# Attention units of one core: where the fp32 products stand among the projections, and where the last output sum and the gate stand

## The chip, the core and the metric

The kernel runs on one core of one Trainium2 chip. The metric is the device time of one execution in microseconds (us). Of three runs the median is 936.8 us, the lowest 935.56 and the highest 937.04.

## What is computed

Four blocks act one after the other on x of shape 64 x 32 x 256 (64 sequences of 32 rows), each added to x: a transformer block with modulation, a GRU, a block attention and an oscillator network. The change touches the transformer block alone, and of it the attention:

```python
x1 = _ln(x) * (1.0 + scale1) + shift1
qkv = (x1 @ qkv_w + qkv_b).reshape(Bc, Tc, 3, H, DH)      # H = 16 heads, DH = 128
q, k, v = (qkv[:, :, 0], qkv[:, :, 1], qkv[:, :, 2])
attn = jnp.einsum('bthd,bshd->bhts', q, k) * scale
attn = jax.nn.softmax(attn, axis=-1)
attn_out = jnp.einsum('bhts,bshd->bthd', attn, v).reshape(Bc, Tc, INNER)
x = x + gate1 * (attn_out @ out_w + out_b)
x2 = _ln(x) * (1.0 + scale2) + shift2
h = jax.nn.gelu(x2 @ ffn_w1 + ffn_b1, approximate=False)
x = x + gate2 * (h @ ffn_w2 + ffn_b2)
```

## The kernel before, in words

The 2048 rows are cut in NG = 4 groups of GT = 512 rows (16 sequences), the 16 heads in NU = 4 units of HU = 4 heads. The attention is software-pipelined over the 16 units (group by group): step U finishes unit U and does the projections of unit U + 1. Each engine has its own program, and semaphores alone tie them.

**TensorE.** A step is a list written out by hand, `STEP` (L477), gone through by `run` (L483). Its entries are:
- `q`, `k` and `v` (`proj`, L390): a projection. Each is a block of six fp32r matmuls of 512 columns (`three`, L349: high times high, low times high, high times low, for two halves of the features). The blocks alternate between two PSUM banks, so a block waits until the block two before it has been copied out (`act_evac`, `dve_evac`).
- `S` (`scores`, L413): the scores of one head, 16 small fp32 matmuls on 32 columns of the array, 32 records in the trace.
- `PV` (`pv`, L425): probabilities by values of one head, four fp32 matmuls of 128 columns, 8 records. It waits for the softmax of its unit at the first head, and for the copies of earlier products.
- `Y` (`head_sum`, L436): the output projection of one head, added up over all 16 heads in two PSUM banks; six fp32r matmuls.

The mean and the variance for the layer norms are one fp32 matmul each by a matrix of 1/256 (two records; four in the first group). `attention` (L549) puts them at the head of a step: `ln_mean(g + 1)` and `ln_var(g + 1)` in steps 0 and 1 of a group; in the last group those of the second norm, `l2_mean(0)`, `l2_var(0)`, `l2_mean(1)`, and `l2_var(1)` at the head of the last step. The last step, `LAST` (L480), has no projections but the first three blocks `U` of the feed-forward (`up`, L512), and the fourth.

**ScalarE** (`attention`, L885) copies out q (`query`, L808) and half of v (`value`, L817), takes the exponential (`exp`, L823), and writes the high part of each head's product (`out_high`, L827). The norm's square, root and high part (`ln_square`, `ln_sqrt`, `high`, or `l2_square`, `l2_sqrt`, `m_high`) stand between `query` 1 and `query` 2.

**VectorE** (`attention`, L1274) copies out k (`key`, L1127) and the other half of v (`value`, L1134), and writes the low part of each product (`out_low`, L1140). Softmax is `soft_a` (L1151: maximum and difference, out of PSUM), `soft_b` (L1159: sum, reciprocal, and the multiplication of the probabilities at L1165, whose operands both lie in SBUF) and `soft_c` (L1167: four transposes of 32 partitions each into the block-diagonal operand `BD` of `PV`). In a step they stand as `soft_a`, `value` 1, `soft_b`, `value` 3, `soft_c`. At the end of a group's last step stands `gate` (L1216): it waits for the last `Y` and adds the gated sum to x, four instructions. The norm's part (`ln_center`, `ln_recip`, `low`, or `l2_center`, `l2_recip`, `m_low`) stands between `key` 1 and `key` 2.

**GpSimd** splits the weights of the units 1 to 3 into high and low parts in the first 101 us (`split`, L1684), and does the modulation of the next group's input (`modulate`, L1667: one multiplication by the reciprocal root, then four of half the size), which starts when VectorE's reciprocal is done. In the last steps it also prepares the feed-forward: the sum of the squares (`sum_squares`, L1704) and the low parts of both weights (`ffn_low`, L1731); the order is written out from L1762 on. `ffn_low(f2_lo, ...)` stands right behind `l2_sum_squares(1)`.

Each engine works through its own list in order: whatever waits holds up all that stands behind it on that engine.

Of the kernel before, what the change touches and what calls it, by code (L numbers as in the profile page):

```python
# [15 lines left out]
NG = 4  # L16
# [83 lines left out]
def build(nc, xT, cond, ada_w, qkv_w, out_w, ffn_w1, ffn_w2, w_ih, w_hh, wk, wo, coup, vecs, out):  # L100
# [20 lines left out]
    with ctx:  # L121
# [224 lines left out]
        def _(pe):  # L346
# [113 lines left out]
            def idle_matmuls(n):  # L460
                for _ in range(n):
# [14 lines left out]
                     ("S", 2), ("v", 0), ("S", 3), ("v", 1), ("v", 2), ("v", 3)]  # L476
            STEP = [("q", 0), ("k", 0), ("q", 1), ("k", 1), ("S", 0), ("q", 2), ("k", 2), ("S", 1), ("PV", 0), ("q", 3),  # L477
                    ("PV", 1), ("k", 3), ("Y", 0), ("S", 2), ("PV", 2), ("Y", 1), ("PV", 3), ("S", 3), ("v", 0),
                    ("Y", 2), ("v", 1), ("v", 2), ("v", 3), ("Y", 3)]
            LAST = [("L", 1), ("U", 0), ("U", 1), ("PV", 0), ("PV", 1), ("U", 2), ("Y", 0), ("PV", 2), ("Y", 1), ("PV", 3),  # L480
                    ("U", 3), ("Y", 2), ("Y", 3)]

            def run(order, U, u, g):  # L483
# [3 lines left out]
                for kind, i in order:  # L487
                    if kind == "PV":
                        pv(U, i)
                    elif kind == "Y":  # L490
                        head_sum(U, u, i, g)
                    elif kind == "U":
                        up(i)
                    elif kind == "L":
                        l2_var(i)
                    elif kind == "S":
                        scores(n, i)
                    else:
                        proj(n, ng, un, (kind, i))
# [48 lines left out]

            def attention(g, last):  # L549
                for u in range(NU):  # L550
                    U = NU * g + u
                    if not last and u == 0:
                        ln_mean(g + 1)
                    if not last and u == 1:
                        ln_var(g + 1)

                    if last and u == 0:
                        l2_mean(0)
                    if last and u == 1:
                        l2_var(0)  # L560
                    if last and u == 2:
                        l2_mean(1)
                    run(LAST if last and u == NU - 1 else STEP, U, u, g)

            for g in range(NG):
                attention(g, g == NG - 1)

# [222 lines left out]
        def _(act):  # L790
# [94 lines left out]
            def attention(g, last):  # L885
                for u in range(NU):
# [3 lines left out]
                    if project:  # L890
                        query(n, un, 0)
                        query(n, un, 1)
                    if u == 0 and not last:
                        ln_square(g + 1)
# [8 lines left out]
                    if u == 2 and last:  # L903
                        m_high(0)
                    if not project:
                        break
                    query(n, un, 2)
                    out_high(U, u, 0)
                    query(n, un, 3)
                    out_high(U, u, 1)  # L910
                    if u == 2 and last:
                        l2_square(1)
                    out_high(U, u, 2)
                    out_high(U, u, 3)
                    value(n, 0)
# [3 lines left out]
            def last_unit():  # L919
                U, u = NU * NG - 1, NU - 1  # L920
                l2_sqrt(1)
                hidden(0)
                hidden(1)
                out_high(U, u, 0)
                out_high(U, u, 1)
                hidden(2)
                out_high(U, u, 2)
                out_high(U, u, 3)
                hidden(3)

# [173 lines left out]
        def _(dve):  # L1104
# [61 lines left out]

            def soft_c(U):  # L1167
                soft_wait(U, "norm")
                dve.wait_ge(pv_done, 1 + 4 * U)
                for j in range(BT):  # L1170
                    js = slice(j * T, j * T + T)
# [102 lines left out]
            def attention(g, last):  # L1274
                for u in range(NU):
# [3 lines left out]
                    if project:  # L1279
                        key(n, un, 0)  # L1280
                        key(n, un, 1)
                    if u == 0 and not last:
                        ln_center(g + 1)
                    if u == 1 and not last:
                        ln_recip(g + 1)
                    if u == 2 and not last:
                        low(g + 1)
                    if u == 0 and last:
                        l2_center(0)
                    if u == 1 and last:  # L1290
                        l2_recip(0)
                    if u == 2 and last:
                        m_low(0)
                        l2_center(1)
                    if not project:
                        break
                    key(n, un, 2)
                    out_low(U, u, 0)
                    out_low(U, u, 1)
                    key(n, un, 3)  # L1300
                    out_low(U, u, 2)
                    out_low(U, u, 3)
                    soft_a(n)
                    value(n, 1)
                    soft_b(n)
                    value(n, 3)
                    soft_c(n)
                    if u == NU - 1:
                        gate(g)

            def last_unit():
                U, u = NU * NG - 1, NU - 1
                hidden_low(0)
                out_low(U, u, 0)
                out_low(U, u, 1)
                l2_recip(1)
                hidden_low(1)
                out_low(U, u, 2)
# [605 lines left out]
```

## Time and profile before

| | |
|---|---|
| median of three runs | 936.8 us |
| the profiled execution, its own time | 935.23 us |
| its span, first to last instruction | 933.5 us |
| TensorE matmul busy | 909.0 us, 97% of the span |
| TensorE weight load busy | 767.8 us, 82% |
| VectorE busy | 613.0 us, 66% |
| ScalarE busy | 415.2 us, 44% |
| GpSimd busy | 258.2 us, 28% |
| chain that ended last | PE 85%, DVE 9%, ACT 3%, issue 2%, DMA 1% |
| the line that holds most of the chain | L355 (the fp32r matmuls), 42% |
| granted TensorE clock, mean | 0.995 of full speed |

The span in 40 slices of 23 us, busy share in tenths:

```profile
PE   7999999999999999999999999999997899999998
DVE  5545645455455455545577885677777988888887
POOL 0655400020000200013502424333214543333333
PEclk9999999999999999999999999999999899999999
```

The attention fills the slices 3 to 21 (from 42.5 to 489.5 us). The profiler's engines are PE (TensorE matmul), PEld (its weight loads), DVE (VectorE), ACT (ScalarE), POOL (GpSimd). Records of matmuls overlap, since they are pipelined: the distance from one start to the next tells what a matmul costs, its own length does not.

### The profile page before, as it was taken

Reading aid. Unit: us, or ns where it says so; the run is one execution under the profiler, and the core shown is the slowest. Engines: PE = TensorE matmul, PEld = TensorE weight load, DVE = VectorE, ACT = ScalarE, POOL = GpSimd, SP = SyncE. Lnnn points to the kernel's source line nnn. Section 1 sums busy time; section 2 is a strip of 40 time slices with the busy share of each in tenths; the row PEclk is TensorE's granted clock in tenths of the full one; section 3 lists DMA queues with packets and bytes.
Section 4 is the critical chain, followed back from the end, with each engine's and each line's share of the span. In section 5 each row is a group of like instructions: output and inputs, shape, how many; then the busy total and the mean of one; then the engine's idle time right before and its main releaser. Section 6 shows DMA issues by size and latency. Waiting matters only on the chain.

```text
span 933.5 us, 18576 instructions
## 1 busy us (share of the span) xinstructions
PE 909.0 (97%) x7254; PEld 767.8 (82%) x7254; DVE 613.0 (66%) x1706; ACT 415.2 (44%) x1147; POOL 258.2 (28%) x344
## 2 busy tenths in 40 slices
PE   7999999999999999999999999999997899999998
PEld 6787887888878888788887778899985599999997
DVE  5545645455455455545577885677777988888887
ACT  3233322333222422224355664555544666666665
POOL 0655400020000200013502424333214543333333
PEclk9999999999999999999999999999999899999999
DMA  8122000000000000110005000000000000000000
GB/s 298 58 74 75 24 1 1 1 2 1 2 1 1 2 1 1 46 46 2 2 1 192 1 0 1 1 2 1 1 2 1 1 2 24 1 24 2 24 2 24
DMA packets 5432, 22.01 MB, mean 24 GB/s; under 512 B 608, under 2 KB 736, under 8 KB 4960
## 3 DMA queue, kind: packets, MB, share of 16 engines
q1 hardware_dynamic: 5344, 20.82, 6.4%
q8 instruction: 57, 0.93, 0.4%
q14 instruction: 31, 0.25, 0.1%
HBM read 18.72 MB, written 2.10 MB: 22 GB/s over the span
## 4 chain that ended last, share of the span: by engine, by line
PE 85%; DVE 9%; ACT 3%; issue 2%; DMA 1%; SPq 0%; POOL 0%; POOLq 0%; DVEq 0%
PE ps L355 42%; PE ps L747 8%; PE ps L432 7%; PE ps L751 7%; PE ps L615 6%; PE ps L746 5%; PE ps L605 3%; PE ps L421 3%; PE ps L617 3%; DVE g_lo L1214 1%; DVE BD L1172 1%; DVE m_lo L1208 1%; DVE frs L1186 1%; DMA BD<-qkv_w 1%; PE ps L622 1%
## 5 line engine op out<-in xcount | busy, mean ns | idle before, releaser
L1142 DVE SCALAR_TENSOR_TENSOR o_lo<-ps,vec,o_hi 128x512 fp32r<-128x512 f32 x64 | 47.9, 750 | 106.4 <-ACT o_hi L830 106.4
L355 PE MATMUL ps<-x_hi,W_hi 128*128 128x512 f32 x256 | 108.6, 424 | 3.4 <-DVE qk L1131 3.0
L355 PE MATMUL ps<-x_lo,W_hi 128*128 128x512 f32 x256 | 100.2, 391 | 0.0
L814 ACT ACTIVATE qk<-ps,vec 128x512 f32<-128x512 f32 x64 | 44.0, 688 | 126.1 <-PE ps L355 126.1
L747 PE MATMUL ps<-rk_th,cpc 128*128 128x128 f32 x512 | 99.0, 296 | 1.1 <-ACT rk_th L1080 1.0
L355 PE MATMUL ps<-x_hi,W_lo 128*128 128x512 f32 x256 | 100.0, 391 | 0.0
L830 ACT ACTIVATE o_hi<-ps,vec 128x512 fp32r<-128x512 f32 x64 | 43.9, 689 | 110.4 <-PE ps L432 110.4
L1131 DVE TENSOR_SCALAR qk<-ps,vec 128x512 f32<-128x512 f32 x64 | 47.4, 740 | 64.9 <-PE ps L355 64.9
L747 PEld LDWEIGHTS ps<-rk_th,cpc 128*128 128x128 f32 x512 | 72.9, 193 | 9.6 <-ACT rk_th L1080 7.3
L746 PE MATMUL ps<-rk_th,cpc 128*128 128x64 f32 x512 | 78.7, 256 | 0.0
L615 PE MATMUL ps<-ht,hh 128*128 128x128 f32 x512 | 77.1, 283 | 0.8 <-DVE ht L1468 0.7
L746 PEld LDWEIGHTS ps<-rk_th,cpc 128*128 128x128 f32 x512 | 73.1, 193 | 0.0
L615 PEld LDWEIGHTS ps<-ht,hh 128*128 128x128 f32 x512 | 66.0, 191 | 7.5 <-DVE ht L1468 4.6
L432 PE MATMUL ps<-BD,V 128*128 128x128 f32 x512 | 70.3, 281 | 0.0
L1080 ACT ACTIVATE rk_th<-rk_q 128x64 f32<-128x64 f32 x192 | 44.5, 253 | 54.0 <-DVE rk_q L1630 22.5
L432 PEld LDWEIGHTS ps<-BD,V 128*128 128x128 f32 x512 | 64.4, 191 | 4.1
L751 PE MATMUL ps<-rk_Z,ident 128*128 128x128 f32 x384 | 64.3, 290 | 0.0
L355 PEld LDWEIGHTS ps<-x_hi,W_hi 128*128 128x128 f32 x256 | 48.2, 188 | 16.3 <-DVE qk L1131 5.0
L355 PEld LDWEIGHTS ps<-x_hi,W_lo 128*128 128x128 f32 x256 | 48.2, 188 | 10.3 <-issue 2.2
L355 PEld LDWEIGHTS ps<-x_lo,W_hi 128*128 128x128 f32 x256 | 48.0, 188 | 10.5
L355 PE MATMUL ps<-W_hi,x_hi 128*128 128x512 f32 x128 | 51.8, 404 | 0.0
L355 PE MATMUL ps<-o_hi,wo_hi 128*128 128x512 f32 x128 | 51.5, 402 | 0.0
(257 smaller groups left out, 2144.1 us busy)
## 6 DMA issues: line engine op xcount, KB each, us to landing
stage<-qkv_w SPq DMA_DIRECT2D x6, 768.0 KB, 4.3
stage<-out_w SPq DMA_DIRECT2D x4, 512.0 KB, 3.8
f_raw<-ffn_w SPq DMA_DIRECT2D x2, 1024.0 KB, 4.8
xorig<-xT SPq DMA_DIRECT2D x1, 2048.0 KB, 8.1
out<-xtb SPq DMA_DIRECT2D x4, 512.0 KB, 3.1
x_all<-xT SPq DMA_DIRECT2D x1, 1536.0 KB, 15.3
ada_sb<-ada_w SPq DMA_DIRECT2D x1, 1024.0 KB, 10.1
BD<-qkv_w SPq DMA_DIRECT2D x1, 768.0 KB, 6.6
```

What stands on the lines that cost most here:

```text
L355: r = pe.matmul(out_, lhsT, rhs, start=first and i == 0, stop=last and i == n - 1)
L421: r = pe.matmul(ps[j * T:j * T + T, SB, (i * HU + h) * T:(i * HU + h) * T + T], qk[:, 0, h % 2, t], qk[:, 1, h % 2, t], start=True, stop=True)
L432: r = pe.matmul(ps[:, OB[h % 2], i * P:i * P + P], V[:, i, h * DH:h * DH + DH], BD[:, i * HU + h, :], start=True, stop=True)
L615: return pe.matmul(ps[:, bank[c], 0:2 * B], hh[:, k, ms], h_.unsqueeze(1).to_broadcast([P, 2, B]), start=k == 0, stop=k == KC - 1)
L746: return pe.matmul(ps[:, RK_BANK[k % 2][c], 0:B], w, th, start=first, stop=last)
L747: return pe.matmul(ps[:, RK_BANK[k % 2][c], 0:2 * B], w, twice(th), start=first, stop=last)
L751: pe.matmul(ps[:, RK_BANK[k % 2][c], 0:2 * B], ident[:, :], twice(rk[z][:, c, :]), start=True, stop=False)
L814: act.activation(qk[:, 0, h % 2, :], ps[:, PJ[0], :], ACT.Identity, bias=col("qkv_b", HU * u + h)).then_inc(act_evac, 1)
L830: act.activation(o_hi[:, h % 2, :], ps[:, OB[h % 2], :], ACT.Identity, bias=col("qkv_b", 2 * HEADS + HU * u + h)).then_inc(ohi_done, 1)
L1080: act.activation(rk[f"th{k % 2}"][:, c, :], rk[src][:, c, :], ACT.Tanh).then_inc(rk_act, 1)
L1131: dve.tensor_scalar(qk[:, 1, h % 2, :], ps[:, PJ[1], :], col("qkv_b", HEADS + HU * u + h), None, ALU.add).then_inc(dve_evac, 1)
L1142: dve.scalar_tensor_tensor(o_lo[:, h % 2, :], ps[:, OB[h % 2], :], col("qkv_b", 2 * HEADS + HU * u + h), o_hi[:, h % 2, :].bitcast(F32), A ...
```

## The change

It puts the fp32 products of a step in two places: both first heads' products by values and scores after the fourth projection block, those of the other two heads after four more projections and two output sums. The fourth output sum `Y` 3 of a unit goes into the next step, after `k` 1 there, and the norm's matmul with it, right behind. On ScalarE and VectorE the orders follow: the norm's work goes behind `query` 3 and `key` 3, `out_high` and `out_low` of the heads 0 and 1 come ahead of `query` 2 and `key` 2, `l2_square(1)` goes behind `out_high` 3, two of the four transposes go ahead of `value` 3, and `gate` goes into the next group's first step, behind `key` 1. The last step changes in the same way.

```diff
-            STEP = [("q", 0), ("k", 0), ("q", 1), ("k", 1), ("S", 0), ("q", 2), ("k", 2), ("S", 1), ("PV", 0), ("q", 3),
-                    ("PV", 1), ("k", 3), ("Y", 0), ("S", 2), ("PV", 2), ("Y", 1), ("PV", 3), ("S", 3), ("v", 0),
-                    ("Y", 2), ("v", 1), ("v", 2), ("v", 3), ("Y", 3)]
-            LAST = [("L", 1), ("U", 0), ("U", 1), ("PV", 0), ("PV", 1), ("U", 2), ("Y", 0), ("PV", 2), ("Y", 1), ("PV", 3),
-                    ("U", 3), ("Y", 2), ("Y", 3)]
+            STEP = [("q", 0), ("k", 0), ("q", 1), ("k", 1), ("previous Y", 3), ("norm", 0), ("PV", 0), ("PV", 1), ("S", 0), ("S", 1),
+                    ("q", 2), ("k", 2), ("q", 3), ("k", 3), ("Y", 0), ("Y", 1), ("PV", 2), ("PV", 3), ("S", 2), ("S", 3),
+                    ("v", 0), ("v", 1), ("Y", 2), ("v", 2), ("v", 3)]
+            LAST = [("previous Y", 3), ("norm", 0), ("U", 0), ("U", 1), ("PV", 0), ("PV", 1), ("U", 2), ("Y", 0), ("Y", 1),
+                    ("PV", 2), ("PV", 3), ("U", 3), ("Y", 2), ("Y", 3)]
...
+                    elif kind == "previous Y":
+                        if U:
+                            head_sum(U - 1, (u - 1) % NU, i, (U - 1) // NU)
+                    elif kind == "norm":
+                        norm_sum(u, g, g == NG - 1)
...
+            def norm_sum(u, g, last):
+                if last:
+                    (l2_mean, l2_var)[u % 2](u // 2)
+                elif u == 0:
+                    ln_mean(g + 1)
+                elif u == 1:
+                    ln_var(g + 1)
```

ScalarE, a step (the norm's lines between are the same as before):

```diff
                     if project:
                         query(n, un, 0)
                         query(n, un, 1)
+                    if not project:
+                        break
+                    out_high(U, u, 0)
+                    out_high(U, u, 1)
+                    query(n, un, 2)
+                    query(n, un, 3)
                     if u == 0 and not last:
                         ln_square(g + 1)
...
-                    if not project:
-                        break
-                    query(n, un, 2)
-                    out_high(U, u, 0)
-                    query(n, un, 3)
-                    out_high(U, u, 1)
+                    out_high(U, u, 2)
+                    out_high(U, u, 3)
                     if u == 2 and last:
                         l2_square(1)
-                    out_high(U, u, 2)
-                    out_high(U, u, 3)
```

VectorE, a step:

```diff
+                    if u == 0 and g:
+                        gate(g - 1)
+                    if not project:
+                        break
+                    out_low(U, u, 0)
+                    out_low(U, u, 1)
                     if u == 0 and not last:
                         ln_center(g + 1)
+                    if u == 0 and last:
+                        l2_center(0)
+                    key(n, un, 2)
+                    key(n, un, 3)
...
                     out_low(U, u, 2)
                     out_low(U, u, 3)
                     soft_a(n)
                     value(n, 1)
                     soft_b(n)
+                    soft_c(n, range(2))
                     value(n, 3)
-                    soft_c(n)
-                    if u == NU - 1:
-                        gate(g)
+                    soft_c(n, range(2, BT))
```

In the last step ScalarE's `out_high` 0 and 1 come ahead of `hidden(0)`, and `out_high` 2 and 3 ahead of `hidden(2)`; VectorE's `hidden_low(0)` comes behind `l2_recip(1)`.

## Rows read from the trace of the kernel before

**Rows 1.** Chain that ended last, in order of time, a plain unit: start us, us, what

```profile
322.11 0.39 PE ps L421 x32
322.49 13.85 PE ps L355 x60
...
340.06 1.09 PE ps L432 x8
...
349.93 0.39 PE ps L421 x32
```

**Rows 2.** The same chain, a unit with a norm's matmul

```profile
436.87 8.41 PE ps L355 x36
445.28 0.86 PE ps L367 x2
```

**Rows 3.** The same chain, the last unit

```profile
477.62 1.78 PE ps L432 x16
479.40 2.99 PE ps L355 x12
...
485.56 8.20 PE ps L355 x36
```

**Rows 4.** Stretches: length, busy us (x) of PE, PEld, DVE, ACT, POOL, PEclk, DMA share, GB/s

```profile
157.60:165.34 7.74, 6.73 (x27) 4.62 (x26) 5.80 (x9) 1.38 (x2) 0.00 (x0) 1.00 0.00 0
416.40:422.83 6.43, 6.43 (x27) 4.70 (x26) 3.00 (x5) 1.92 (x3) 0.87 (x1) 1.00 0.36 146
93.32:107.47 14.16, 14.15 (x69) 11.11 (x61) 9.92 (x13) 4.90 (x7) 9.87 (x8) 1.00 0.12 38
```

**Rows 5.** Timeline of DVE, end of the first group: start, us, what, count [idle before]

```profile
157.05 2.89 DVE L1172 STREAM_TRANSPOSE BD<-Pr 32x512 f32<-32x512 f32 x4
160.05 0.75 DVE L1224 SCALAR_TENSOR_TENSOR Pr<-ps,vec,ada 128x512 f32<-128x512 f32 x1
...
162.96 0.74 DVE L1131 TENSOR_SCALAR qk<-ps,vec 128x512 f32<-128x512 f32 x1
```

**Rows 6.** Timeline of PE, a unit with the norm's root

```profile
212.27 0.39 PE L355 MATMUL ps<-W_hi,x_hi 128*128 128x512 f32 x1
```

**Rows 7.** Timeline of ACT, the same unit

```profile
193.52 1.28 ACT L802 ACT_TABLE_LOAD   x1
...
209.73 0.60 ACT L821 ACTIVATE V<-ps 128x512 f32<-128x512 f32 x1 [1.29 <-PE ps L355]
...
211.64 0.63 ACT L825 ACTIVATE Pr<-Pr 128x512 f32<-128x512 f32 x1
```

**Rows 8.** Timeline of DVE, the same unit

```profile
195.54 3.35 DVE L1121 RECIPROCAL rs<-rs 128x512 f32<-128x512 f32 x1 [0.61 <-ACT rs L802]
...
212.47 0.69 DVE L1138 COPY V<-ps 128x512 f32<-128x512 f32 x1 [1.92 <-PE ps L355]
213.08 0.68 DVE L1161 TENSOR_REDUCE sm<-Pr 128x16 f32<-128x512 f32 x1
...
214.08 0.69 DVE L1165 TENSOR_TENSOR Pr<-Pr,sm 128x512 f32<-128x512 f32 x1
```

**Rows 9.** Timeline of POOL, the same unit: the modulation

```profile
198.97 2.39 POOL L1670 TENSOR_TENSOR xc<-xc,rs 128x1024 f32<-128x1024 f32 x1 [29.19 <-DVE rs L1121]
201.44 4.20 POOL L1675 TENSOR_TENSOR xc<-xc,ada 128x512 f32<-128x512 f32 x4
```

**Rows 10.** Timeline of POOL, then of DVE, at the end of the second unit

```profile
98.67 2.40 POOL L1689 TENSOR_TENSOR wo_lo<-stage,wo_hi 128x1024 fp32r<-128x1024 f32 x1
...
99.36 2.27 DVE L1165 TENSOR_TENSOR Pr<-Pr,sm 128x512 f32<-128x512 f32 x1
```

**Rows 11.** Timeline of ACT, then of POOL, in the fifteenth unit

```profile
459.34 1.05 ACT L856 ACTIVATE fsq<-fc 128x1024 f32<-128x1024 f32 x1
...
460.47 1.29 POOL L1706 TENSOR_TENSOR fsq<-fsq 128x512 f32<-128x512 f32 x1 [9.98 <-ACT fsq L856]
461.72 4.57 POOL L1734 TENSOR_TENSOR f_lo<-f_raw,f_hi 128x2048 fp32r<-128x2048 f32 x1
```

More of the change, by code:

```diff
@@ L493, in run @@
                         up(i)
-                    elif kind == "L":
-                        l2_var(i)
+                    elif kind == "previous Y":
[3 more added lines that the diff above has]
+                        norm_sum(u, g, g == NG - 1)
                     elif kind == "S":
@@ L547, in down @@
                     r.then_inc(down_done, 1)
[L549 to L566, printed above, removed]
+            def norm_sum(u, g, last):
[5 more added lines that the diff above has]
+                    ln_var(g + 1)
+            for U in range(NU * NG):
+                run(LAST if U == NU * NG - 1 else STEP, U, U % NU, U // NU)
             down(0)
@@ L921, in last_unit @@
                 l2_sqrt(1)
+                out_high(U, u, 0)
+                out_high(U, u, 1)
                 hidden(0)
                 hidden(1)
-                out_high(U, u, 0)
-                out_high(U, u, 1)
-                hidden(2)
                 out_high(U, u, 2)
                 out_high(U, u, 3)
+                hidden(2)
                 hidden(3)
@@ L1165, in soft_b, with soft_c @@
                 dve.tensor_tensor(Pr[:, :, :], Pr[:, :, :], sm[:, :].unsqueeze(2).to_broadcast(whole), ALU.mult).then_inc(soft, 1)
-            def soft_c(U):
+            def soft_c(U, blocks=range(BT)):
                 soft_wait(U, "norm")
                 dve.wait_ge(pv_done, 1 + 4 * U)
-                for j in range(BT):
+                for j in blocks:
                     js = slice(j * T, j * T + T)
@@ L1287, in attention @@
                         low(g + 1)
-                    if u == 0 and last:
-                        l2_center(0)
                     if u == 1 and last:
@@ L1294, in attention @@
                         l2_center(1)
[L1295 to L1300, printed above, removed]
                     out_low(U, u, 2)
@@ L1305, in attention @@
                     soft_b(n)
+                    soft_c(n, range(2))
                     value(n, 3)
-                    soft_c(n)
-                    if u == NU - 1:
-                        gate(g)
+                    soft_c(n, range(2, BT))
             def last_unit():
                 U, u = NU * NG - 1, NU - 1
-                hidden_low(0)
                 out_low(U, u, 0)
@@ L1316, in last_unit @@
                 l2_recip(1)
+                hidden_low(0)
                 hidden_low(1)
```

## The prediction

> **What bounds the kernel.** I read the page first: TensorE is busy for 97% of the span and holds 85% of the chain. So I went on to the chain in order of time, inside the attention. Through a plain unit it runs on TensorE without a break, 27.82 us from one unit's last scores to the next's [rows 1]. What shortens it is less on TensorE, or fewer waits; the other engines count only where TensorE waits for them.
>
> The reader is to see in [rows 1] that a piece's price depends on what it follows. 36 fp32r matmuls behind a `PV` take 8.20 us, 0.228 each [rows 3]. The 60 behind an `S` take 13.85 where 60 x 0.228 is 13.67, and 36 behind one take 8.41, 0.21 more than 8.20 [rows 2]. A `PV` behind `S` takes 1.09, two in a row 1.78, 0.89 each [rows 3], so 0.20 less. Leaving scores costs about 0.2 us; `S` itself is 0.39.
>
> **The change part by part.** *The regrouping.* Four departures from scores in a unit become two. The new unit, in pieces that rows show: behind the last `S` again 60 (`v` 0, `v` 1, `Y` 2, `v` 2, `v` 3, `q` 0, `k` 0, `q` 1, `k` 1, `Y` 3), 13.85; two pairs of `PV`, 2 x 1.78; 36 behind `S`, 8.41; four `S`, 1.55. Sum 27.37, against 27.82: 0.45 less, in 15 units 6.7 us. No row shows `S` behind `S`. Within one head 32 records follow each other in 0.39 us, and the next head is more of them: I take nothing extra. Nothing less either, since that 0.39 holds no departure; above, a full departure, 0.2 in 30 places, 6.0 us.
>
> *The norm's matmul* moves and is kept, 0.86 us [rows 2]. It now stands between `Y` and `PV`. The 36, the matmul and the 24 that follow make up about 0.04 more than 13.85 and 0.86, so at most 0.4 us for nine places goes or comes: I count zero.
>
> *The last step* has its `PV` in two pairs (1.78 as the row's pair, so nothing) and loses a wait ahead of `Y` 0: 12 matmuls took 2.99 [rows 3] where 12 x 0.228 is 2.73. ScalarE now writes the high parts ahead of `hidden(0)`. Gain 0.3.
>
> *The gate.* It waits for `Y` 3 at a group's end, and VectorE runs it from 160.05 to 162.96, with the next `key` 0 behind it [rows 5]; `k` 1 waits for that copy. The stretch from the norm's matmul to the first scores is 7.74 us in such a step and 6.43 where no gate stands [rows 4]: 1.31, in three places 3.9 us. Behind `key` 1 the gate begins when `Y` 3 ends, about 7.0 us into the unit, and ends at 9.9. Behind it wait `out_low` 0, `out_low` 1 and `ln_center`, up to 12.6; `key` 2 is wanted at 13.4 (seven blocks of 1.36, the norm's 0.9, two `PV` and two `S` 2.6, a departure 0.2, and 0.2 until a copy begins), `Y` 0 at 16, which also needs the two sum banks that the gate has read. So it is hidden, with 0.8 us to spare; without that cover it would cost TensorE what it cost before.
>
> *The third unit's 60* took 14.16 [rows 4] against 13.85, behind a late softmax: 0.3 may go, but see the rule below; I count it.
>
> Gains together: 6.7 + 0.3 + 3.9 + 0.3 = 11.2 us.
>
> *The new waits.* The last projection of `v` leaves its bank through VectorE's `value` 3, now behind `soft_b` and two transposes (half of 2.89 [rows 5], 1.45). The next `k` 0 needs that bank. I work it through for the steps with the norm's root (the second of each group), counting from the end of block `k` 3:
> - A copy begins 0.20 after its block ends (212.27 to 212.47 [rows 6, 8]). So `query` 3 begins at -1.16, the table load at about -0.45, the reciprocal 2.02 later [rows 7, 8], at 1.57, and the modulation on GpSimd 3.43 after that [rows 8, 9], at 5.0. Its first instruction is followed after 2.47 by four in 4.20 [rows 9]: the last of them runs from 10.6 to 11.7.
> - On TensorE `Y` 0 and `Y` 1 (2.7), `PV` 2 and 3 (1.8), `S` 2 and 3 (0.8) and `v` 0 (1.6) end at 6.9. The copy begins at 7.1, the exponential 1.91 later with a table load between [rows 7], ends 9.6; the sum begins at 9.7 and the multiplication L1165 1.00 later [rows 8], at 10.7.
> - Undisturbed it ends at 11.4, two transposes at 12.8, `value` 3 at 13.5; `k` 0 is wanted at 13.7 (five blocks behind `v` 0). No wait, with 0.2 to spare.
>
> But two instructions that read SBUF twice over collide: at 99.36 the multiplication took 2.27 instead of 0.69 and ended at 101.63, 0.56 after GpSimd's (98.67 + 2.40) [rows 10]. In the steps above it comes 0.1 us after GpSimd's last one began. Held to 11.7 it ends at 12.2, `value` 3 at 14.4: `k` 0 waits 0.7. Three groups (units 6, 10, 14; in the first, GpSimd is still at the weights): 2.2 us. Had it come 0.1 earlier, it would take its turn between two of them: nothing. I take the 2.2, by the step's own arithmetic, and keep zero as the other end.
>
> *The fifteenth unit.* `l2_square(1)` is moved behind `out_high` 3, so that it ends about 6.4 after `k` 3 (1.05 long); the sum of squares takes 1.29, and the low part of the second weight, one instruction of 4.57 us [rows 11], runs from 7.7 to 12.3. No table load here, so the multiplication is ready at 10.0, held to 12.3, ends at 12.9; two transposes, 14.3; `value` 3, 15.0. The last step's `U` 0 needs it and is wanted at 14.5 (four blocks, `Y` 3 and 0.86): 0.5 us. It is 2.3 us deep inside the other instruction, so I count it; the other end is zero.
>
> Moved without a price: `high`, `low`, `m_high`, `m_low` (done at about 17 of 27 us, wanted by the next unit); the transposes, which `PV` 0 now wants some 6 us after they end; no DMA is moved, and SP's queue waits for projections, which come earlier.
>
> **Sum.** 11.2 - 2.2 - 0.5 = 8.5 us. The profiled execution took 935.2 and would take 926.7; the median stands 1.6 above it, so 928.3.
>
> **A rule weighed.** The row shows a TENSOR_TENSOR of GpSimd blocking [rows 10]. The Trainium skill (SBUF — State Buffer, Who interferes with whom) says that a VectorE instruction with two SBUF inputs contends with any GpSimd instruction that reads SBUF, and that the loser blocks to the end. This trace agrees for the pair shown; a TENSOR_SCALAR against it no row here shows.
>
> **The rivals.**
> 1. *The multiplication slips in ahead* of GpSimd's last instruction. For it: the distance is 0.1 us over a chain of 12 us. Then 2.2 comes back: 926.1. Chance 0.28.
> 2. *GpSimd's scalar form blocks too.* In the second unit I put the multiplication at about 97.8, when GpSimd is at the instruction just ahead of that at 98.67. Held to 98.6, it ends at 99.2, `value` 3 comes 0.6 late, the third unit waits as long: 928.9. Were it 0.9 later still, it would meet the next one and cost 2 more. By the rule just named this is what happens. Chance 0.20.
> 3. *Scores behind scores cost a departure:* 6.0 more, 934.3. Against it: the 32 even records. Chance 0.05.
> 4. *The gate's wait comes back* behind `out_low` and `key` 2, 3 x 1.3: 932.2. It needs VectorE 0.8 us later than counted. Chance 0.05.
> 5. *Slower.* `value` 3 behind the two transposes holds `k` 0 in all 15 units. It decides where VectorE is later by more than 0.5 us in plain steps and 0.2 in those with the root; it turns the sign at 11.2 / 15 = 0.75 of wait a unit, so some 1.3 us late. If both transposes and the multiplication met such delays everywhere (1.6 us as in [rows 10], less the 0.5), that is 1.1 x 15 = 16.5 us against 11.2: 942. Against it: GpSimd is idle in most units. Chance 0.04.
> 6. *It does less than it says*, TensorE waiting elsewhere for about what it gains, within 0.2%: chance 0.05.
>
> **How the numbers follow.** The forecast has 0.33. The likeliest is 928.3. Measurement can tell about 0.2% (1.9 us) from no change. Faster by more than that: the forecast and rivals 1, 2, 4 and, at 934.3 just so, most of 3: 0.90. Same 0.06, slower 0.04. For the range: down to rival 1 less the 0.4 of the norm, the 0.5 of the fifteenth unit and part of the clock's play; up past rival 2 with its further 2 us, towards rival 4. The clock's play is this: the page's granted clock shows one slice of 8, from 723 to 747 us, in a later stage where TensorE waits; 0.1 to 0.2 of those 23 us is 2 to 4 us at the lower rate, and shifted by 8 us the dip may fall better or worse, an estimate of 1 to 2 us. 924.3 to 932.
>
> **What would show it.** Chain: `PV` x16 twice and `S` x64 at 0.78 in a unit; 27.4 for a plain unit; no `Pr L1224` in it. Stretch ahead of the first `S` in a group's first step: no wait of TensorE for `qk L1131`. Waits: three of 0.7 on `V L1138` ahead of `k` 0, one of 0.5 ahead of `U` 0; on VectorE three L1165 of 1.5 us and one near 3. A plain unit over 27.6 would prove the regrouping wrong; waits of TensorE in plain units, rival 5.

## The result and the profile after

The changed kernel takes **924.4 us** (922.4 to 927.1 in four executions) against 936.9 us (of four executions; the 936.8 above is of three): ratio 0.9872, interval 0.9859 to 0.9885, a gain of 12.5 us where 8.5 were forecast. The profiled execution took 922.4 us, with a span of 920.7; before it was 935.2 and 933.5.

Two measures serve below. A *chain piece* is read as before the prediction. A *start-to-start* length runs from the first record of one piece to the first of the next; in these a plain unit before is 27.82 us. The *attention* is the time from the first record of scores to the last record of a product, start to start: 456.09 us before, 443.06 after. The difference is 13.0 us, so the whole gain lies there; the rest adds and takes a few tenths (448.7 us of the trace lie behind the attention's last product, before 448.2), and the spans end 12.8 apart.

The page after, span, busy times and the slices' row of the granted clock:

```profile
span 920.7 us, 18591 instructions
PE 901.2 (98%) x7254; PEld 771.7 (84%) x7254; DVE 615.9 (67%) x1706; ACT 414.4 (45%) x1147; POOL 260.0 (28%) x344
...
PEclk9999999999999999999999999999998999999999
```

TensorE runs the same 7254 matmuls in 12.8 us less and is still busy nearly throughout. The slice of lower clock now lies at 690 to 713 us; it was at 723 to 747.

The chain in order of time, a plain unit after (start us, us, what), which answers to [rows 1]:

```profile
312.62 0.69 PE ps L421 x50
313.31 13.87 PE ps L355 x60
327.18 1.78 PE ps L432 x16
328.96 0.69 PE ps L421 x50
329.66 8.38 PE ps L355 x36
338.04 1.78 PE ps L432 x16
339.82 0.69 PE ps L421 x50
```

From 312.62 to 339.82 it is 27.20 us with a wait of 0.05 in its 60 (they follow a root); start to start a plain unit is 27.16, **0.66 less** than before. The two runs of scores take 0.69 each (all 64 matmuls; the chain lists 50 of them), and the forecast had 0.78. One head by itself takes 0.39 start to start, the pair 0.69, so the second head's scores behind the first's cost 0.31, not 0.39.

The chain in a group's first step, which answers to the first of [rows 4]:

```profile
146.80 13.82 PE ps L355 x60
160.62 0.86 PE ps L367 x2
161.48 1.78 PE ps L432 x16
```

TensorE does not wait. The timeline of VectorE over the same time shows the gate behind a `key` copy, with TensorE past it:

```profile
159.30 0.75 DVE L1126 TENSOR_SCALAR qk<-ps,vec 128x512 f32<-128x512 f32 x1 [1.97 <-PE ps L355]
160.66 0.75 DVE L1219 SCALAR_TENSOR_TENSOR Pr<-ps,vec,ada 128x512 f32<-128x512 f32 x1 [0.61 <-PE ps L355]
```

The waits by engine and line show the three waits for a `key` copy (before 3.0 us) gone, and two others inside the attention (us in total, times, the longest): at the last step's `U` 0, and at the first step's `k` 1:

```profile
PE ps L355 <- DVE V L1133: 0.6, 1, 0.6
...
PE ps L355 <- DVE qk L1126: 0.3, 1, 0.3
```

The second is a cost of the change that the forecast does not have. The chain shows it:

```profile
45.95 0.76 DVE qk L1126
...
46.75 1.66 PE ps L355 x6
```

VectorE's copies of the first unit stand ahead of its loop, and there all four transposes are still behind `value` 3 (`soft_c(0)`); the `key` copy comes behind them. Before, the norm's matmul of four records stood at the head of the step, between `v` 3 and `q` 0, and gave time; now it stands behind `k` 1, and no `Y` 3 of a unit ahead is there. So the first step is 0.07 us shorter than before, from its last scores to the next unit's, where a plain one is 0.66 shorter: a loss of **0.6 us**. (The 0.3 of the list is what the engine is idle by its records, which overlap.)

The two collisions that the forecast counted. The timeline after of VectorE, then of GpSimd: a unit with the norm's root (the first row of each) and the fifteenth unit (the second of each). *Blocked* means that an instruction takes longer because the other engine's is under way:

```profile
208.04 0.69 DVE L1160 TENSOR_TENSOR Pr<-Pr,sm 128x512 f32<-128x512 f32 x1
...
456.40 2.88 DVE L1160 TENSOR_TENSOR Pr<-Pr,sm 128x512 f32<-128x512 f32 x1
...
204.96 4.69 POOL L1671 TENSOR_TENSOR xc<-xc,ada 128x512 f32<-128x512 f32 x4
...
454.12 4.61 POOL L1730 TENSOR_TENSOR f_lo<-f_raw,f_hi 128x2048 fp32r<-128x2048 f32 x1
```

In the first the multiplication ran in its 0.69 us and GpSimd's group of four took 4.69 in place of 4.20 [rows 9]: its last instruction began at 208.10, 0.06 **behind** the multiplication, and it was the one blocked (1.54 us instead of 1.05). The same order, by 0.05 to 0.06, stands in the other two such units. TensorE's 60 matmuls took 13.79, 13.78 and 13.81 there, against 13.73 in a plain unit: 0.2 us in all where 2.2 were counted. In the fifteenth unit the multiplication came 2.3 us deep inside the other and took 2.88.

### The profile page after: what moved, and what is told of

Read it like the earlier page. It is cut to its first block, busy times and chain, and to the rows that moved or that the text cites. A ratio compares the mean times of both kernels' runs of the same rounds, so it can differ in the third digit from the quotient of the medians.

```text
span 920.7 us, 18591 instructions
## 1 busy us (share of the span) xinstructions
PE 901.2 (98%) x7254; PEld 771.7 (84%) x7254; DVE 615.9 (67%) x1706; ACT 414.4 (45%) x1147; POOL 260.0 (28%) x344
## 4 chain that ended last, share of the span: by engine, by line
PE 87%; DVE 8%; ACT 3%; issue 1%; POOL 0%; POOLq 0%; DVEq 0%; ACTq 0%
PE ps L355 43%; PE ps L742 8%; PE ps L746 6%; PE ps L610 6%; PE ps L432 6%; PE ps L741 5%; PE ps L600 3%; PE ps L612 3%; PE ps L421 2%; PE ps L617 1%; DVE g_lo L1209 1%; DVE m_lo L1203 1%; PE ps L367 1%; DVE frs L1181 1%; PE ps L362 1%
## 5 line engine op out<-in xcount | busy, mean ns | idle before, releaser
L355 PE MATMUL ps<-x_hi,W_hi 128*128 128x512 f32 x256 | 102.0, 399 | 0.7 <-DVE x_lo L1254 0.4
L432 PEld LDWEIGHTS ps<-BD,V 128*128 128x128 f32 x512 | 62.1, 191 | 6.1 <-issue 4.3
L432 PE MATMUL ps<-BD,V 128*128 128x128 f32 x512 | 62.3, 275 | 0.0
L355 PEld LDWEIGHTS ps<-x_lo,W_hi 128*128 128x128 f32 x256 | 48.1, 188 | 10.3
L746 PEld LDWEIGHTS ps<-rk_Z,ident 128*128 128x128 f32 x384 | 50.6, 192 | 0.3 <-DVE rk_Z L1609 0.3
```

What stands on the lines that cost most here:

```text
L355: r = pe.matmul(out_, lhsT, rhs, start=first and i == 0, stop=last and i == n - 1)
L432: r = pe.matmul(ps[:, OB[h % 2], i * P:i * P + P], V[:, i, h * DH:h * DH + DH], BD[:, i * HU + h, :], start=True, stop=True)
L746: pe.matmul(ps[:, RK_BANK[k % 2][c], 0:2 * B], ident[:, :], twice(rk[z][:, c, :]), start=True, stop=False)
```

## The experiments

Three questions stand: what the regrouping is worth and why it gave more than its pieces; whether moving the gate and `Y` 3 gives anything; and whether the collisions of VectorE and GpSimd are what the forecast took them for. My theory after the result, as the expectations have it: a sum of parts, 0.66 us in each of 15 units from the regrouping, and 3.9 us from the gate's move on top. The other view: the regrouping alone gives it all. Attention lengths, start to start, of every profiled execution:

| kernel | attention us | less than before |
|---|---|---|
| before | 456.09 | |
| the change, three executions | 443.06, 444.13, 442.97 | 13.0, 12.0, 13.1 |
| gate moved alone | 451.87 | 4.2 |
| regrouping alone | 442.61 | 13.5 |
| the change, one pair of scores split | 448.57 | 7.5 |
| the change, transposes whole | 450.46 | 5.6 |
| the change, square earlier | 442.70 | 13.4 |
| the change, three small writes ahead of the product | 443.15 | 12.9 |
| the change, product made later | 446.12 | 10.0 |
| regrouping, `Y` 2 ahead of `v` 1 | 445.82 | 10.3 |
| regrouping, transposes whole | 445.59 | 10.5 |
| regrouping, square earlier | 441.86 | 14.2 |

### The change again

> The changed kernel once more, beside the others on one chip. Theory A (the gain is made of three sums that show in the trace: 0.66 us less in each of 15 units, 1.3 us in three steps with a gate, 0.3 in the third unit, less 0.8 of waiting ahead of U 0 in the last step): 13.0 us less inside the attention, ratio to before 0.986. Theory B (part of the median's gain is the clock's, since its four runs lie at 922.4, 922.7, 926.1 and 927.1): again two levels some 4 us apart, and a profile of a run at the upper level shows the loss behind the attention.

924.0 us (922.3 to 927.5 in four), ratio 0.9883 (0.9859 to 0.9908); a third series, run beside other kernels, is below. The profiled execution took longer, span 925.8. The stretches view of its first projections (length, PE busy, clock, DMA share, GB/s):

```profile
20.00:32.00 12.00, 9.18 (x76) 0.86 0.17 63
```

The granted clock is 0.86 in the mean there (a part of the stretch at the lower level, 1.2 GHz, the rest at 2.4), where both first profiles have 1.00: the first 24 matmuls took 7.26 us instead of 5.81, and attention began 2.1 us later. The attention is 1.1 longer, and what lies behind it 1.9 longer (450.6 us against 448.7); together these are the 5.1 between the spans. At the end of the second unit, the timeline of VectorE, then of GpSimd:

```profile
99.75 1.62 DVE L1160 TENSOR_TENSOR Pr<-Pr,sm 128x512 f32<-128x512 f32 x1
...
98.42 2.40 POOL L1685 TENSOR_TENSOR wo_lo<-stage,wo_hi 128x1024 fp32r<-128x1024 f32 x1
100.78 2.83 POOL L1666 TENSOR_TENSOR xc<-xc,rs 128x1024 f32<-128x1024 f32 x1
```

Here GpSimd, which follows a transfer, is ahead of the attention by more, and its next instruction holds the multiplication: 1.62 us instead of 0.69. It then took its turn as soon as the first had ended, and GpSimd's following one paid 0.43. The third unit's 60 matmuls took 14.75, 1.0 more than in a plain unit. This collision is worth a microsecond, and whether it happens varies: of the twelve profiled executions of the changed kernel and its variants (the gate moved alone left out) the second unit's multiplication was blocked in five. Expected were 13.0 us less inside the attention; it was 12.0, by this collision.

> The changed kernel once more. Theory A (startup shifts TensorE's first projection by up to 2 us against GpSimd's weight splitting, which the loads set): where the trace shows the first projection as late as 40.1 us (fourth scores), the second unit's multiplication meets GpSimd's split and the third unit's 60 matmuls take 14.7 us; where it is at 38, 13.8 us. Theory B: the level of a run is set by how long the clock is at half where TensorE is thin, near 715 and 730 us and in the first projection, 3.4 or 6.8 us each time.

925.4 us (923.1 to 928.9 in four), ratio 0.9896 (0.9871 to 0.992). The profiled one took 923.1; its third unit shows 13.79 and the three units with the root 13.79, 13.77 and 13.77: the multiplication at 209.16, GpSimd's last at 209.23. So the order of 0.06 us holds in all three profiles of this kernel; in each the multiplication begins 5.69 to 5.70 us behind the start of the last scores. The fourth scores began at 38.7 and the second unit did not collide, which agrees with the expectation. But a late start alone does not bring the collision: in the run with three small writes, below, they began at 39.8 and the stretch took 13.81, for there GpSimd waited longer for its transfer and came after the multiplication (99.86 against 99.77).

### The gate moved alone

```diff
# kernel before, VectorE
                         l2_center(1)
+                    if u == 0 and g:
+                        gate(g - 1)
...
                     soft_c(n)
-                    if u == NU - 1:
-                        gate(g)
```

> The kernel before with the gate alone moved: out of the end of a group's last step into the next group's first step, behind ln_center; scores, products and Y 3 stay where they were. Theory A: the wait of k 1 on the copy behind the gate goes in three places, 3.9 us less, about 933.0 where before is 936.9; a plain unit stays at 27.82 us. Rival (the gate only moves its wait: out_low 0, key 2 or the next Y 0 pay): within 1 us of before.

931.8 us (931.3 to 932.5), ratio 0.9962 (0.9947 to 0.9977). The chain in a group's first step:

```profile
158.90 0.86 PE ps L367 x2
159.76 5.48 PE ps L355 x24
165.24 0.39 PE ps L421 x32
```

The 24 matmuls run without a wait: start to start 5.98 where before it was 7.28, 1.30 in each of three places, 3.9 us. The third unit's 60 gave 0.3 more in this execution (13.85). A plain unit stays at 27.82. So the term of 3.9 us holds, taken by itself.

### The regrouping alone

```diff
# changed kernel
-            STEP = [("q", 0), ("k", 0), ("q", 1), ("k", 1), ("previous Y", 3), ("norm", 0), ("PV", 0), ...
+            STEP = [("norm", 0), ("q", 0), ("k", 0), ("q", 1), ("k", 1), ("PV", 0), ...
...
-                    ("v", 0), ("v", 1), ("Y", 2), ("v", 2), ("v", 3)]
+                    ("v", 0), ("v", 1), ("Y", 2), ("v", 2), ("v", 3), ("Y", 3)]
...
-                    if u == 0 and g:
-                        gate(g - 1)
...
                     soft_c(n, range(2, BT))
+                    if u == NU - 1:
+                        gate(g)
```

> The changed kernel with Y 3 and the norm's matmul back at the step's end and head and the gate back at the group's end: the regrouping alone. Theory A: a unit of 27.16 us, 15 x 0.66 = 9.9 us less, the three waits of 1.3 us for the copy behind the gate are there again, about 926.5 to 927.5. Rival (Y 3 in the next step is what makes room for the pairs): TensorE waits for out_low or the softmax in plain units, the unit stays above 27.5 us and the time above 931.

923.2 us (921.8 to 925.1), ratio 0.9868 (0.9846 to 0.989): **all of the gain, without `Y` 3's move and the gate's**. The attention is even 0.45 us shorter than with them, mostly since the first step's loss of 0.6 us is not there either. I had expected three waits of 1.3 us and 926.5 to 927.5: that was wrong. The timeline of VectorE at the end of the first group tells why no gate is felt:

```profile
151.51 0.69 DVE L1133 COPY V<-ps 128x512 f32<-128x512 f32 x1 [0.85 <-PE ps L355]
...
155.59 0.69 DVE L1133 COPY V<-ps 128x512 f32<-128x512 f32 x1 [0.32 <-PE ps L355]
156.31 1.44 DVE L1167 STREAM_TRANSPOSE BD<-Pr 32x512 f32<-32x512 f32 x2
157.86 0.75 DVE L1219 SCALAR_TENSOR_TENSOR Pr<-ps,vec,ada 128x512 f32<-128x512 f32 x1
...
160.77 0.74 DVE L1126 TENSOR_SCALAR qk<-ps,vec 128x512 f32<-128x512 f32 x1
```

The gate takes the same 2.9 us ahead of the `key` copy, but begins 1.35 us earlier against the matmuls (9.41 us behind the end of the last scores, before 10.76). `v` 1 stands ahead of `Y` 2, so that its copy and the softmax behind it come one block of 1.36 earlier, and two transposes are then already done ahead of `value` 3. `v` 3 itself ends no earlier. The 24 matmuls took 5.92, 5.92 and 5.89. Of the units with the root, the two whose 60 stand undivided took 13.73: with `Y` 3 behind `v` 3, `k` 0 comes 1.36 us later and `value` 3 has that much time to spare.

### Which part of the new order removes the gate's wait

```diff
# regrouping alone
-                    ("v", 0), ("v", 1), ("Y", 2), ("v", 2), ("v", 3), ("Y", 3)]
+                    ("v", 0), ("Y", 2), ("v", 1), ("v", 2), ("v", 3), ("Y", 3)]
```

> The regrouping alone with Y 2 ahead of v 1 again, as before the change. In the regrouping alone the gate at the group's end costs nothing: the stretch behind the norm's matmul takes 5.89 to 5.92 us. Theory A (v 1 ahead of Y 2 lets VectorE copy v 1 and finish the softmax 1.3 us earlier, so the gate is over when k 0's copy is wanted): with Y 2 first, value 1, the sum and the multiplication come 0.8 to 1.3 us later, and k 1 waits 0.3 to 1.0 us in the three steps with a gate. Rival (the split of the transposes alone did it): 5.9 us as before.

925.3 us, one execution. The chain ahead of the first scores of the second group:

```profile
158.28 0.76 DVE Pr L1219
...
159.68 0.76 DVE qk L1126
...
160.48 1.66 PE ps L355 x6
```

The gate is in the chain again and six matmuls (`k` 1) follow the copy; the 24 took 6.93, 6.94 and 6.93: 1.01 to 1.04 more in three places. Here the transposes come 1.36 later and end after `v` 3, so that `value` 3 waits for them.

```diff
# regrouping alone
                     soft_b(n)
-                    soft_c(n, range(2))
                     value(n, 3)
-                    soft_c(n, range(2, BT))
+                    soft_c(n)
```

> The regrouping alone with all four transposes behind value 3. Theory A: the gate begins 1.2 us later (at the end of transposes that start when value 3 ends), key 0 too, and k 1 waits about 1.0 us in each of the three steps with a gate (24 matmuls 6.9 us instead of 5.9); plain steps keep 27.16, since Y 3 stands between v 3 and q 0 here. Rival (the order of v 1 and Y 2 alone did it): 5.9 us as before.

926.9 us, one execution. The 24 matmuls took 7.18, 7.19 and 7.19: 1.3 more each. The wait at the fifteenth unit is gone in it, 0.8 less, and the attention is 3.0 longer, as 3.8 less 0.8 would have it. Either half of the order, undone, brings nearly the whole wait back, so both are needed where the gate isn't moved.

### Transposes whole, with `Y` 3 moved

The same edit on the changed kernel.

> The changed kernel with all four transposes behind value 3, as before the change. Theory A (the split spreads VectorE's load so that neither value 3 nor key 0 comes late): the four end about 0.7 us later than key 0 is wanted, k 1 waits for the bank about 0.3 us in every step, the unit goes from 27.16 to about 27.5, 4 to 5 us in all. Rival (value 3 comes earlier and k 0 gains what k 1 loses): the same within 1 us.

932.8 us, one execution. Now **every** unit waits. The chain, at the head of a plain unit:

```profile
358.59 0.71 DVE BD L1167
359.33 0.76 DVE qk L1126
360.14 1.89 PE ps L355 x7
```

`k` 1 waits for a `key` copy behind four transposes; the 60 matmuls took 14.33 to 14.35, 0.6 more in each of the 14 such stretches, twice what I had expected. That is 8.4 us; the wait at the last step's `U` 0 (0.8) is gone with it, and the attention is 7.4 longer than in the change. In the run before this, with `Y` 3 in its place, the same transposes cost plain units nothing (13.73). That is the price of the move of `Y` 3: it takes away 1.36 us of cover at the seam of every unit, and only the split of the transposes makes up for it. It is rival 5's mechanism, at a price of 0.6 a unit, just under the 0.75 that would have turned the sign.

### One pair of scores split

```diff
# changed kernel
-                    ("PV", 0), ("PV", 1), ("S", 0), ("S", 1), ("q", 2), ("k", 2), ...
+                    ("PV", 0), ("PV", 1), ("S", 0), ("q", 2), ("S", 1), ("k", 2), ...
```

> The changed kernel with the first pair of scores taken apart: S 1 behind q 2, all else as it is. Theory A, sharpened by the trace after (two S in a row take 0.69 us, not 2 x 0.39, and each stay apart also pays an entry of 0.07 and a departure of 0.15): 0.31 us more a unit, 15 x 0.31 = 4.6 us more than the changed kernel. The prediction's own pricing (0.39 for each S wherever it stands, 0.2 for a departure): 3.0 us more. Rival (the number of places does not matter, only waits do): no difference.

929.7 us (928.9 to 930.0), ratio 0.9938 (0.9923 to 0.9952). The chain of a plain unit:

```profile
335.19 0.39 PE ps L421 x32
335.58 1.59 PE ps L355 x6
337.17 0.39 PE ps L421 x32
337.56 7.03 PE ps L355 x30
```

Start to start, 0.388 + 1.590 + 0.388 + 6.940 = 9.31, where the pair and the 36 take 0.693 + 8.292 = 8.99: 0.32 in this unit, 0.31 in the mean of 15, 4.7 us. The attention is 5.5 longer; 0.9 of that is a collision in the second unit (the third unit's 60 took 14.68), as in the change run again. One more place of scores costs **0.31 us**: 0.08 that only the first of them pays (0.388 less 0.305) and 0.22 to 0.24 more in the fp32r matmuls that follow (1.590 + 6.940 - 8.292 in this unit).

### The fifteenth unit's square

```diff
# changed kernel, ScalarE
-                    out_high(U, u, 2)
-                    out_high(U, u, 3)
                     if u == 2 and last:
                         l2_square(1)
+                    out_high(U, u, 2)
+                    out_high(U, u, 3)
```

> The changed kernel with l2_square(1) alone back ahead of out_high 2. Theory A: as above, the wait of 0.8 us ahead of U 0 goes (the norm's two records and 12 matmuls 3.6 us instead of 4.4), nothing else changes. Rival: unchanged, or out_high 2 and 3 come late and Y 2 waits for them.

923.5 us (921.1 to 927.4), ratio 0.9867 (0.9844 to 0.9891). The norm's matmul and the 12 behind it took 0.455 + 3.166 = 3.62, against 1.58 + 2.84 = 4.42 in the change: the 0.80 is gone. The long instruction of GpSimd now runs 452.65 to 457.28 and the multiplication, 0.38 us ahead of its end, took 0.92 instead of 2.88. The attention is only 0.4 shorter, for in this execution the second unit collided, with GpSimd's **scalar** form. The timeline of VectorE, then of GpSimd:

```profile
97.67 1.24 DVE L1160 TENSOR_TENSOR Pr<-Pr,sm 128x512 f32<-128x512 f32 x1
...
97.31 1.06 POOL L1683 TENSOR_SCALAR wo_hi<-stage 128x1024 fp32r<-128x1024 f32 x1 [4.00 <-DMA stage<-out_w]
```

GpSimd came 0.36 us first; the multiplication took 1.24 us, and the third unit's 60 took 14.33, 0.6 more. In the profile of the change the order at this place is the other way round, on the timeline of VectorE, then of GpSimd:

```profile
97.61 0.69 DVE L1160 TENSOR_TENSOR Pr<-Pr,sm 128x512 f32<-128x512 f32 x1
...
97.64 1.57 POOL L1683 TENSOR_SCALAR wo_hi<-stage 128x1024 fp32r<-128x1024 f32 x1 [3.83 <-DMA stage<-out_w]
```

VectorE came first by 0.03, and GpSimd paid 0.51 us that nobody waits for.

### The multiplication made later

> The changed kernel with three small memsets (about 0.2 us together) ahead of the multiplication L1160 in the units 6, 10 and 14. Theory A (the instruction that comes first holds the way to SBUF to its end, and the change's VectorE came first by 0.06 us): GpSimd's last instruction of the modulation goes first, takes 1.05 us instead of 1.54, the multiplication takes about 1.5 instead of 0.69, and k 0 waits about 1.0 us more in each of the three steps, their 60 matmuls taking 14.7 to 14.9 us instead of 13.79. Rival (both share the way, and 0.2 us of delay costs 0.2 us): 60 matmuls in 14.0 us.

```diff
# changed kernel, units 6, 10 and 14
+                 if U > NU and U % NU == 2 and U < NU * NG:
+                     for i in range(3):
+                         dve.memset(eps_t[:, 2 * i + 1:2 * i + 3], LN_EPS)
```

923.9 us, one execution; the stretches 13.83, 13.81 and 13.82. It settles nothing: the writes began together with the multiplication, at 210.27, and against the matmuls it came only 0.03 to 0.04 us later than in the change, still 0.02 to 0.03 ahead of GpSimd's last instruction. With two small reductions in their place it is delayed:

```diff
+                     for i in range(2):
+                         dve.reduce_max(mx[:, 4 * i:4 * i + 4], ones[:, :].rearrange("p (a b) -> p a b", b=32), axis=AX.X)
```

> Two small VectorE reductions (128 elements each, of a constant into a sum's dead buffer) stand ahead of the multiplication in units 6, 10 and 14, so that it begins some 0.2 to 0.4 us later and GpSimd's last modulation instruction, 0.06 us behind it before, is first. Theory (whoever is first keeps the port, the other is blocked to its end): in those three units the multiplication takes 1.4 to 1.6 us instead of 0.69, GpSimd's instruction 1.05 instead of 1.54, and the next step's first 60 fp32r matmuls take 14.6 to 14.9 us in place of 13.79: each 0.8 to 1.1 more, in all 2.4 to 3.2 us, 927 to 928. Rival (TensorE has slack there and the collision costs nothing whichever way it falls): the three stretches stay at 13.8 to 14.0 and the time at 924 to 925.

925.5 us, one execution. The timeline of VectorE, then of GpSimd:

```profile
208.20 0.48 DVE L1162 TENSOR_REDUCE mx<-ones 128x4 f32<-128x128 f32 x2
208.59 1.26 DVE L1163 TENSOR_TENSOR Pr<-Pr,sm 128x512 f32<-128x512 f32 x1
...
205.11 4.20 POOL L1674 TENSOR_TENSOR xc<-xc,ada 128x512 f32<-128x512 f32 x4
```

GpSimd's group is back at its 4.20 us and the multiplication takes 1.26: the loser has changed. The 60 matmuls took 14.81, 14.76 and 14.75 against 13.79, 13.78 and 13.81, 0.98 more each on average, and the attention 446.12, 3.06 more than 443.06. Counted from the start of the last scores, the multiplication ended 0.97 us later than in the change, 0.40 of it its later start and 0.57 the block, and TensorE lost all of it. That refutes the rival in this run's text: there is no slack on TensorE's side. The stretches came out as my theory had them; the whole time, 925.5, is 1.5 us under the least that it gave, which one execution can't tell from the spread (the spans of the two profiles, 923.7 and 920.7, are 3.0 apart).

### The best version

The regrouping alone, with the square ahead of `out_high` 2.

> The regrouping alone (Y 3 and the norm's matmul at the step's end and head, the gate at the group's end), and l2_square(1) back ahead of out_high 2, so that GpSimd's one long instruction of 4.6 us is over before the fifteenth unit's multiplication. Theory A: that multiplication takes 0.69 us instead of 2.88, and the 0.8 us of waiting ahead of U 0 goes; 0.8 us less than the regrouping alone, a median near 922.5, below both kernels. Rival (the long instruction only moves onto another VectorE instruction that reads SBUF twice, or U 0 waits for m_low instead): no gain over the regrouping alone.

**921.9 us** (920.8 to 923.0 in five), ratio 0.9849 (0.9835 to 0.9862). The chain in the last step:

```profile
459.66 0.86 PE ps L367 x2
460.52 2.76 PE ps L355 x12
463.29 1.78 PE ps L432 x16
```

No wait ahead of `U` 0, none in the units with the root (13.73), none for the gate (5.92, 5.92, 5.89), and an attention of 441.86: 1.2 us less than the change and 0.75 less than the regrouping alone. The attention is what ranks them; the whole times of the regrouping with and without the square overlap. GpSimd's long instruction still meets the multiplication, which took 0.91 us. It needs neither `previous Y` nor the gate in another group's step.

## Why the prediction was right, and where not

**The sign and the bound** were right: TensorE's chain set the time, and the gain is in the attention. **The number** was 3.9 us off. 924.4 lies 0.1 inside the range's lower end, 924.3, and the second series, 924.0, lies outside it: that the range holds is luck. Most of what brought the time down there is the cheaper second head's scores (2.5 us) and the collisions that did not come (2.0 us of 2.2), which the forecast had only as rival 1.

**The regrouping** was counted 6.7 us and measured 0.66 x 15 = 9.9. The step that failed is "No row shows `S` behind `S` ... I take nothing extra. Nothing less either". A second head's scores behind the first's cost 0.305 where 0.388 were taken: 0.17 a unit, 2.5 of the 3.2 us missing. The 32 even records that I read show that scores run evenly within a head; they don't show what the first of them costs, and that is not paid a second time. The rest, 0.05 a unit, is 0.7: fp32r matmuls and products together took 25.77 start to start, 0.50 less than before where I had 0.45. The direct test, one pair split, gave 0.31 a place. *The norm's matmul*, which I counted at zero, gave about 0.04 us in each of eight places, 0.3 in all, of the 0.4 that I allowed.

**The gate** gave the 3.9 us as counted (1.30 three times), and its new place is free of waits, so rival 4 did not come. But the prediction credits the move, and the regrouping alone shows that the other edits remove the same wait. The move and the regrouping, 4.2 and 13.5 us by themselves, make 13.0 together. What I had not worked through is VectorE's order at the seam: two transposes ahead of `value` 3, which the forecast had under the things "moved without a price", and `v` 1 ahead of `Y` 2, of which it says nothing, are worth 3.8 and 3.1 us where the gate stays, and the first 0.6 a unit where it and `Y` 3 go.

**The last step** gave its 0.3: from `U` 2 to the norm's matmul behind the last sum 14.14 us start to start, where it was 14.44. **The third unit** gave 0.3 in this profile and lost 0.7 in the one run again. **The first step** lost 0.6 that the forecast does not have: it reckoned with the new order of the transposes everywhere, but the first unit's stand ahead of VectorE's loop and stayed whole.

**The new waits with the root** were counted 2.2 and cost 0.2. Mechanism and price are real (0.98 each when GpSimd is first, where 0.7 was counted; the 0.2 us of room that I had given `k` 0 is not there, for even undisturbed those units wait 0.06), but the order was the other one: rival 1 came true. I had the multiplication 0.1 us behind GpSimd's last instruction, and it was 0.06 ahead. The cheaper pair of scores between `k` 3 and `v` 0, 0.085, may be half of that 0.16; no run separates it. A step-by-step sum over 12 us can't settle such an order; both signs should have had about the same chance. Once the program stands, though, the order is fixed: it is the same in every profile with this order of the softmax.

**The fifteenth unit** cost 0.80 where 0.5 was counted; the multiplication began 2.28 us inside the other, as the prediction had it, and ended 0.55 after it (459.28 against 458.73). The step that was short is the one behind: `value` 3 ends at 461.47 and `U` 0 begins 0.14 later, which I had left out, and TensorE was there 0.1 earlier against GpSimd. Moving the square back removes the wait.

**Rival 2** has the right mechanism: GpSimd's scalar form contends too, at 0.6 us, the price that I gave. It was blocked rather than blocking in the profile of the change, and blocking in that of the earlier square. The Trainium skill (SBUF — State Buffer, Who interferes with whom) has any GpSimd instruction that reads SBUF contend with a VectorE instruction of two SBUF inputs; these rows agree, in both directions. **Rival 3** is refuted, with the opposite sign: scores behind scores cost less, not more. **Rival 5** needed waits in all units; there were none in plain ones, but undoing the split of the transposes calls them up.

In sum, for the attention of this profile: 9.9 + 3.9 + 0.3 + 0.3 + 0.3 - 0.2 - 0.8 - 0.6 = 13.1 against 13.0 measured. What differs between executions of the same kernel, up to 6.6 us, is partly the clock at the start (1.5 us, in attention that began 2.1 later), partly whether the second unit collides (0.6 to 1.0); the rest falls behind the attention, where stretches at the lower clock lie at different places in each profile. That last part I have only seen, not tested.

## What to carry to other kernels

Where matmuls of two shapes alternate on TensorE, count the changes of shape, and price them by a run that merges or splits one place: the first of a kind pays, the ones behind it don't. At a seam, the place between two steps, where one engine empties a bank for the next step, put only what the bank needs ahead of it; a block of TensorE's work moved away from there takes its cover with it. Before a change takes up two moves against one wait, try each alone: here either was enough.

## What the runs showed of the hardware

- Scores (32 columns of the array, 32 elements wide) following scores cost 0.31 us a head, the first 0.39, and leaving them for fp32r matmuls 0.22 to 0.24. The first fp32r matmul behind scores is followed by the next after 0.34 us, where two in a row are 0.23 apart. The Trainium skill (TensorEngine Tiling (Array Packing), Key Properties) says that a change of the tiling mode drains TensorE. The trace agrees with a cost at each such change: 0.31 us for going in and out once more.
- Of VectorE's multiplication with two SBUF inputs and a GpSimd instruction that reads SBUF, the later one pays; a lead of 0.03 to 0.06 us was enough. It paid what was left of the other less 0.14 or 0.15: VectorE 0.57 and 0.55 (of 0.72 and 0.70), GpSimd 0.49 and 0.51 (of 0.63 and 0.66). In the change run again, GpSimd's next instruction came behind the multiplication that had waited.
- Three small writes ahead of a multiplication on VectorE started within 0.02 us of it and put it off by 0.03 to 0.04, two reductions of 128 elements per partition put it off by 0.4.
- The granted clock from 20 to 32 us was 1.00 in the profile of the change and 0.86 in that of the same kernel run again, worth 1.5 us at the first 24 matmuls of the projections.
